# A preparing pass over the context, dissolved into two cross attentions of a four-layer kernel

## The reference, cut to what matters

```
L0 cross attention: 16 heads of 64, keys and values projected from ctx
L1 cross attention:  8 heads of 64, keys and values projected from layernorm(ctx) * g + b
L2 cross attention, linear: k = ctx @ wk, v = ctx @ wv                   (256 x 256 each)
    k' = (relu(layernorm(k) * g + b) + 1e-6) * mask
    v' = (layernorm(v) * g + b) * mask
    kv = k'^T v' over all 12544 rows, and the sum of k' over the rows; both small
```

## Time and profile before

| What | Value |
|---|---|
| median of 3 executions | 3282.53 us (3282.21 to 3284.53) |
| profiled execution, its own time | 3287.21 us |
| its span, first to last instruction | 3285.6 us |
| busy PE, DVE, ACT, POOL | 2809.3, 1830.1, 1530.2, 475.2 us |
| mean granted TensorE clock | 0.927 |
| preparing stage | about 3.5 to 347.4 us |
| first cross attention | about 348 to 1533 us |
| second cross attention | about 1737 to 2365 us |
| HBM read, written | 201.27 MB, 38.80 MB |

### The profile page before, as it was taken

The page is one execution under the profiler, slowest core; times in us unless marked ns, Lnnn a source line. Parts: engine busy times, 40 slices in busy tenths (PEclk is TensorE's granted clock), DMA queues, the critical chain, the costliest instruction groups (busy, mean ns, idle before and its releaser), DMA issues. The chain is left out here.

```text
span 3285.6 us, 72653 instructions
## 1 busy us (share of the span) xinstructions
PE 2809.3 (86%) x26026; PEld 2244.3 (68%) x26026; DVE 1830.1 (56%) x5010; ACT 1530.2 (47%) x3126; POOL 475.2 (14%) x915
## 2 busy tenths in 40 slices
PE   6788699999999999995666999999767559999973
PEld 5666588888888888884345888888546446777752
DVE  7999455555555555554574555555453347565625
ACT  5777455555555555552443555555300002444441
POOL 3333111111111111100012222222000011000000
PEclk9999899999999999997787999999869687999985
DMA  3334311111111111001442111110124264334210
GB/s 112 119 119 118 114 57 42 39 36 35 35 35 35 35 35 35 29 2 36 163 156 86 35 35 35 35 35 22 55 110 166 107 248 128 123 114 125 75 35 18
DMA packets 128243, 244.15 MB, mean 74 GB/s; under 512 B 16448, under 2 KB 89168, under 8 KB 122576
## 3 DMA queue, kind: packets, MB, share of 16 engines
q1 hardware_dynamic: 95696, 208.26, 18.9%
q10 hardware_dynamic: 28672, 19.27, 1.9%
q0 software_dynamic: 3584, 12.58, 1.2%
HBM read 201.27 MB, written 38.80 MB: 73 GB/s over the span
## 5 line engine op out<-in xcount | busy, mean ns | idle before, releaser
L340 PE MATMUL l0x_psum<-l0x_fast 128*128 128x448 f32 x1344 | 331.6, 383 | 20.3 <-DVE l0x_fast L545 12.8
L470 ACT ACTIVATE l0x_sbuf<-l0x_sbuf 128x896 f32<-128x896 f32 x224 | 233.2, 1041 | 231.2 <-DVE l0x_sbuf L565 231.2
L1447 DVE CUSTOM_DVE_ANT_0 l3x_sbuf<-l3x_psum,l3x_fast,l3x_sbuf 128x896 f32<-128x896 f32 x224 | 253.4, 1150 | 140.0 <-PE l3x_psum L1294 135.6
L1378 ACT ACTIVATE l3x_sbuf<-l3x_psum 128x512 f32<-128x512 f32 x392 | 213.7, 596 | 220.7 <-PE l3x_psum L1313 220.2
L355 PE MATMUL l0x_psum<-l0x_fast 128*128 128x512 f32 x1176 | 310.5, 401 | 0.9 <-POOL l0x_fast L625 0.9
L551 DVE TENSOR_TENSOR l0x_fast<-l0x_psum,l0x_fast 128x448 fp32r<-128x448 f32 x224 | 140.0, 625 | 298.3 <-ACT l0x_fast L450 298.3
L340 PEld LDWEIGHTS l0x_psum<-l0x_fast 128*128 128x128 f32 x1344 | 237.2, 190 | 41.8 <-issue 12.9
L565 DVE CUSTOM_DVE_ANT_0 l0x_sbuf<-l0x_psum,l0x_sbuf 128x896 f32<-128x896 f32 x224 | 248.9, 1149 | 25.6 <-PE l0x_psum L369 25.6
L186 PE MATMUL prep_psum<-prep_sbuf 128*128 128x256 f32 x784 | 196.8, 395 | 70.0 <-DMA prep_sbuf<-in_ctxT 63.8
L576 DVE COPY l0x_sbuf<-l0x_psum 128x384 f32<-128x384 f32 x224 | 124.8, 557 | 236.3 <-PE l0x_psum L386 236.3
L355 PEld LDWEIGHTS l0x_psum<-l0x_fast 128*128 128x128 f32 x1176 | 213.5, 188 | 57.3 <-issue 16.7
(11 more groups left out here) (700 smaller groups left out, 5625.7 us busy)
## 6 DMA issues: line engine op xcount, KB each, us to landing
l3x_fast<-ctx_high SPq DMA_DIRECT2D x112, 224.0 KB, 3.7
l1f_sbuf<-in_L_ffn_W SPq DMA_DIRECT2D x16, 1024.0 KB, 6.8
l2f_sbuf<-in_L_ffn_W SPq DMA_DIRECT2D x16, 1024.0 KB, 6.9
prep_sbuf<-in_ctx_rows SPq DMA_DIRECT2D x98, 128.0 KB, 2.1
prep_sbuf<-in_ctxT SPq DMA_DIRECT2D x98, 128.0 KB, 2.5
xnT<-prep_sbuf ACTq DMA_DIRECT2D x98, 128.0 KB, 2.3
l0x_sbuf<-in_ctxT SPq DMA_DIRECT2D x14, 896.0 KB, 6.2
ctx_high<-l0x_fast SPq DMA_DIRECT2D x14, 896.0 KB, 7.8
```

The lines of the kernel that those rows point to most:

```text
L340: mm = pe.matmul(ps[:, 0:width], self.wk[w][:, c, pr * T:(pr + 1) * T], x[:, c, lo:lo + width], start=(j == 0), stop=(j == len(products) - 1))
L470: act.activation(self.p[:, (2 * m + a) % 4, 0:width], self.sm[:, a, 0:width], ACT.Exp, scale=-1.0, bias=self.negm[:, n % 2, 2 * pr + a:2 * ...
L1378: act.activation(p[:, u % 4, :, :, :].rearrange("p h a t -> p (h a t)"), ps_t[slot["tiles", u]][:, :], ACT.Exp).then_inc(s.sem("p"), 1)
L1447: dve.tensor_tensor_reduce(junk[:, a, :].rearrange("p (i c) -> p i c", i=2), ps_s[a][:, :, 0:HALF], bias[:, n * CH:(n + 1) * CH].bitcast(F ...
```

## The change

The preparing stage is gone from `STAGES`. Its work moves:

- **Into the first cross attention**, in a new class `ContextSide`. Per tile one column group of 512 columns in f32r, key and value weights of the linear attention side by side (three products of two halves, as for the values), one in each of the steps pr 0 to 6. ACT empties it. DVE takes three `bn_stats` at the end of that step. Twice a chunk (tiles 0 to 3 and 4 to 6) DVE aggregates, forms the inverse roots by a shift, a constant and three Newton steps (`dve_scales`, ends of pr 4 and pr 7), and normalises keys and values (`dve_normal`, ends of pr 5 and of pr 0 of the next chunk). POOL applies gain, shift and relu to the keys of the batch (ends of pr 5 and pr 0). PE forms the sums of a batch at the end of pr 7 and of pr 3 of the next chunk, in one of the two shared banks, and DVE adds that bank to a running total one step later, behind its first L551.
- The output weights `wo` get the place of the side's keys and values, so they are loaded when the last sums are done. Raw weights lie in other buffers, and `v` is kept for four pairs of heads at a time instead of eight.
- **Into the second cross attention**: it reads `ctxT` and the means and inverse spreads of the rows, which the first one writes to HBM (49 KB each). Per chunk SP loads them to all partitions (448 KB each), and POOL does three operations on each of the two halves of 896 columns (`norm_part`), at pr 1 for the chunk after the next. At the start POOL does one half of chunk 0 and DVE the other, and POOL all of chunk 1 before its first `diff`.
- In both attentions the groups of chunk 0 are no longer ahead of step 0, but in the steps 0 and 1 (and for the first attention's second half of the heads in 2 to 5).

```diff
+        for u in range(self.M // 4):
+            n, e = divmod(u, P // 4)
+            steps = range(4 * u - 2, 4 * u + 2) if u else range(2)
+            mine = [(n, t, e) for t in range(self.tiles(n))]
             for i, m in enumerate(steps):
                 lo, hi = i * len(mine) // len(steps), (i + 1) * len(mine) // len(steps)
-                self.plan[m] = [len(self.groups) + k for k in range(lo, hi)]
+                self.plan.setdefault(m, []).extend(("v", len(self.groups) + k, 0) for k in range(lo, hi))
             self.groups += mine
-        uses = [("k", 0, i) for i in range(len(self.halves(0)))] + [("v", g, 0) for g in self.plan[-1]]
+            self.ready.append(len(self.groups))
+        if side is not None:
+            for n in range(NCH):
+                for t in range(CT):
+                    self.plan.setdefault(P * n + t, []).append(("side", n * CT + t, 0))
+        uses = [("k", 0, i) for i in range(len(self.halves(0)))]
         for m in range(self.M + 2):
             keys = [("k", m + 1, i) for i in range(self.parts_of(m + 1))]
-            groups = [("v", g, 0) for g in self.plan.get(m, [])]
+            groups = self.plan.get(m, [])
             turns = [("turn", m - 2, 0)] if m >= 2 else []
-            uses += keys[:1] + groups[:1] + keys[1:] + groups[1:] + turns
+            sums = [("sum", b, 0) for b in side.sums_at(m)] if side is not None else []
+            uses += keys[:1] + groups[:1] + keys[1:] + groups[1:] + turns + sums
         self.slot = {use: i % 2 for i, use in enumerate(uses)}
         self.before = {use: uses[i - 2] for i, use in enumerate(uses) if i >= 2}
 
...
-        for g in self.plan[-1]:
-            self.pe_group(pe, g)
...
+            if self.side is not None:
+                for b in self.side.sums_at(m):
+                    self.side.pe_sum(pe, b, self.pe_slot(pe, "sum", b, 0))
...
-        act.wait_ge(s.sem("raw_in"), (n + 1) * 16)
+        if self.norm_dram is None:
+            act.wait_ge(s.sem("raw_in"), (n + 1) * 16)
+        else:
+            act.wait_ge(s.sem("normed"), 2 * n + 2)
...
             if m + 1 < self.M:
                 self.dve_keys(dve, m + 1, 0)
+            if self.side is not None:
+                for b in self.side.sums_at(m - 1):
+                    self.side.dve_summed(dve, b, self.ps_kv[self.slot["sum", b, 0]])
...
                 self.dve_turned(dve, m - 1, 1)
             if m >= 2:
                 self.dve_acc(dve, m - 2)
+            if self.side is not None:
+                self.side.dve_step(dve, m)
...
+    def norm_part(self, eng, n, c):
+        s = self.s
+        eng.wait_ge(s.sem("raw_in"), (n + 1) * 16)
+        eng.wait_ge(s.sem("mean_in"), (n + 1) * 16)
+        eng.wait_ge(s.sem("rstd_in"), (n + 1) * 16)
+        eng.wait_ge(s.sem("gain_in"), 32)
+        part = self.raw[:, c, :]
+        eng.tensor_tensor(part, part, self.mean[:, :], ALU.subtract).then_inc(s.sem(f"centered{c}"), 1)
+        eng.wait_ge(s.sem(f"centered{c}"), n + 1)
+        eng.tensor_tensor(part, part, self.rstd[:, :], ALU.mult).then_inc(s.sem(f"scaled{c}"), 1)
+        eng.wait_ge(s.sem(f"scaled{c}"), n + 1)
+        eng.tensor_scalar(part, part, self.gain[:, 0, c:c + 1], self.gain[:, 1, c:c + 1], ALU.mult, ALU.add).then_inc(s.sem("normed"), 1)
+
+    def pool_norm(self, pool, n):
+        for c in range(DC):
+            self.norm_part(pool, n, c)
...
+            if pr == 1 and self.norm_dram is not None and n + 2 < NCH:
+                self.pool_norm(pool, n + 2)
+            if self.side is not None:
+                self.side.pool_step(pool, m)
+        if self.side is not None:
+            self.side.pool_step(pool, self.M)
...
+    def sums_at(m):
+        n, pr = divmod(m, 8)
+        if pr == 7 and 0 <= n < NCH:
+            return [2 * n]
+        if (pr == 3 and 0 < n < NCH) or (pr == 1 and n == NCH):
+            return [2 * n - 1]
+        return []
+
+    @staticmethod
+    def tiles(b):
+        return range(4) if b % 2 == 0 else range(4, CT)
...
+    def act_in(self, act, i, ps):
+        s = self.s
+        n, t = divmod(i, CT)
+        act.wait_ge(s.sem("side_ps"), i + 1)
+        self.wait(act, "sum_ps", 2 * n - (1 if t < 4 else 0))
+        act.activation(self.kv[:, t, :].rearrange("p (b e) -> p b e", b=2)[:, :, 0:D],
...
+    def dve_step(self, dve, m):
+        n, pr = divmod(m, 8)
+        if n < NCH and pr < CT:
+            self.dve_moments(dve, n, pr)
+        if n < NCH and pr == 4:
+            self.dve_scales(dve, 2 * n)
+        if n < NCH and pr == 5:
+            self.dve_normal(dve, 2 * n)
+        if n < NCH and pr == 7:
+            self.dve_scales(dve, 2 * n + 1)
+        if n > 0 and pr == 0:
+            self.dve_normal(dve, 2 * n - 1)
+
+    def dve_moments(self, dve, n, t):
+        s = self.s
+        dve.wait_ge(s.sem("side"), n * CT + t + 1)
+        dve.wait_ge(s.sem("rows_in"), (n + 1) * 16)
+        self.wait(dve, "side_mv", n * 3 * CT - (9 if t < 4 else 0))
+        dve.bn_stats(self.st[:, t, 0, :], self.k(t)).then_inc(s.sem("side_st"), 1)
+        dve.bn_stats(self.st[:, t, 1, :], self.v(t)).then_inc(s.sem("side_st"), 1)
+        dve.bn_stats(self.st[:, t, 2, :], self.rows[:, t, :]).then_inc(s.sem("side_seen"), 1)
+    def dve_scales(self, dve, b):
+        s = self.s
+        mine, n = slice(self.tiles(b)[0], self.tiles(b)[-1] + 1), b // 2
+        dve.wait_ge(s.sem("side_st"), 2 * self.seen(b))
+        dve.wait_ge(s.sem("side_seen"), self.seen(b))
+        self.wait(dve, "side_v", b - 1)
+        for t in self.tiles(b):
+            for i in range(3):
+                dve.bn_aggr(self.mv[:, t, i, :], self.st[:, t, i, :]).then_inc(s.sem("side_mv"), 1)
+        dve.wait_ge(s.sem("side_mv"), 3 * self.seen(b))
+        dve.wait_ge(s.sem("side_ready"), 3)
+        link = linker(dve, s.sem("side_steps"), 12 * b)
+        var, half, r = self.var[:, mine, :], self.half[:, mine, :], self.r[:, mine, :]
+        link(dve.tensor_tensor(var, self.mv[:, mine, :, 1], self.eps[:, mine, :], ALU.add))
+        link(dve.tensor_scalar(half.bitcast(I32), var.bitcast(I32), 1, None, ALU.logical_shift_right))
+        link(dve.tensor_scalar(r.bitcast(I32), half.bitcast(I32), -1.0, 1597463007.0, ALU.mult, ALU.add))
+        for _ in range(3):
+            link(dve.scalar_tensor_tensor(out=half, in0=r, scalar=-0.5, in1=r, op0=ALU.mult, op1=ALU.mult))
+            link(dve.tensor_tensor(half, half, var, ALU.mult))
+            link(dve.scalar_tensor_tensor(out=r, in0=half, scalar=1.5, in1=r, op0=ALU.add, op1=ALU.mult))
+        at = slice(n * CT + mine.start, n * CT + mine.stop)
+        if b == 0:
+            dve.wait_ge(s.sem("side_squares"), 1)
+        dve.tensor_tensor(self.scale[:, mine], self.r[:, mine, 1], self.masks[:, at, 1], ALU.mult).then_inc(s.sem("side_scale"), 1)
+        dve.tensor_copy(self.stats[:, 0, at], self.mv[:, mine, 2, 0]).then_inc(s.sem("side_stats"), 1)
+        dve.tensor_copy(self.stats[:, 1, at], self.r[:, mine, 2]).then_inc(s.sem("side_stats"), 1)
+
+    def dve_normal(self, dve, b):
+        s = self.s
+        dve.wait_ge(s.sem("side_scale"), b + 1)
+        for t in self.tiles(b):
+            ins = dve.tensor_scalar(self.k(t), self.k(t), self.mv[:, t, 0, 0:1], self.r[:, t, 0:1], ALU.subtract, ALU.mult)
+        ins.then_inc(s.sem("side_z"), 1)
+        for t in self.tiles(b):
+            ins = dve.tensor_scalar(self.v(t), self.v(t), self.mv[:, t, 1, 0:1], self.scale[:, t:t + 1], ALU.subtract, ALU.mult)
+        ins.then_inc(s.sem("side_v"), 1)
+
+    def dve_summed(self, dve, b, ps):
+        s = self.s
+        dve.wait_ge(s.sem("sum_ps"), b + 1)
+        dve.wait_ge(s.sem("side_ready"), 3)
+        self.wait(dve, "summed", b)
+        dve.tensor_tensor(self.total[:, :, :], self.total[:, :, :], ps[:, 0:260].rearrange("p (c e) -> p c e", c=2),
+                          ALU.add).then_inc(s.sem("summed"), 1)
...
+    def pool_step(self, pool, m):
+        s = self.s
+        n, pr = divmod(m, 8)
+        if pr == 4:
+            self.wait(pool, "sum_ps", 2 * n)
+            for at in (D, self.W + D):
+                pool.tensor_copy(self.kv[:, :, at:at + 2], self.masks[:, n * CT:(n + 1) * CT, :]).then_inc(s.sem("side_masks"), 1)
+        b = 2 * n if pr == 5 else 2 * n - 1
+        if pr == 5 or (pr == 0 and n > 0):
+            k = self.kv[:, self.tiles(b)[0]:self.tiles(b)[-1] + 1, 0:D]
+            gain, shift = (v[:, :].unsqueeze(1).to_broadcast([128, len(self.tiles(b)), D]) for v in (self.g, self.b))
+            pool.wait_ge(s.sem("side_z"), b + 1)
+            pool.tensor_tensor(k, k, gain, ALU.mult).then_inc(s.sem("side_gained"), 1)
+            pool.wait_ge(s.sem("side_gained"), b + 1)
+            pool.tensor_tensor(k, k, shift, ALU.add).then_inc(s.sem("side_shifted"), 1)
+            pool.wait_ge(s.sem("side_shifted"), b + 1)
+            pool.tensor_scalar(k, k, 0.0, 1e-6, ALU.max, ALU.add).then_inc(s.sem("side_k"), 1)
+
+    def pe_sum(self, pe, b, ps):
```

(27 more changed lines are left out.)

408 lines of the change are left out of this document (160 added, 248 removed).

## The result

The changed kernel takes 3545.5 us (median of 4 runs, 3539.9 to 3554.8), the kernel before 3283.5 (4 runs, 3282.2 to 3288.1): a ratio of 1.080, 95% interval 1.077 to 1.082. It is slower by 262 us. The forecast was 3317, with a range of 3230 to 3390: the sign was right, the size was not.

The account below looks back on a forecast made before the run. DVE bounds the preparing stage, PE both cross attentions. Stage removed -343.9, first attention +329, second attention's POOL work +44, its start +6: +35 us, 3322, or 3317 against the median; range 3230 to 3390.

Parts of the forecast that it names:

- the forecast's 13.2 us of products: First attention, PE: 98 side groups at 1.36 us, 133 us, and 392 sum products, 52 us; together +185.
- forecast (10.2, and the 0.9 of before): First attention's seams: DVE work and bank order make PE wait 10.2 us a chunk, 141 us in all.
- 3.7 us of DVE work at pr 5 and 3.0 at pr 0: First attention's seams: moments and normalising on DVE, making PE wait 2.0 us at pr 5 and 0.6 at pr 0.
- POOL's batches: First attention: three operations of 1024 or 768 elements, some 7 us in a step of 11 or more, costing nothing.
- costs of nothing: First attention: ACT's 98 copies, POOL's side operations and SP's row loads were all claimed to add no time.
- my bounds for that term: First attention's seam waits: lower 7 us a chunk (98 in all), upper 13 (181), by how far DVE operations overlap.
- a forecast of 3.7: Second attention: POOL's 10.5 us of normalising delays `diff` and `alpha`; PE waits 3.7 us a chunk, 44 in 12 chunks.
- The waits at pr 4, pr 7 and pr 3: First attention's seams: PE waits 3.2 us for DVE's scales chain, 2.4 and 2.0 for the sum's bank.
- the seam's room of 1.7 us: Between two steps of the first attention, DVE has 1.7 us free; work beyond it delays PE one for one.
- the bank's order: First attention, pr 3: PE waits 2.0 us for the sum's bank, freed only behind L551, though DVE is idle enough.
- rival 1: First attention's seams: DVE overlaps its short operations, waits 98 us instead of 141, kernel 3274; chance 0.32.
- Rival 2: Second attention: POOL's batch is the dear one, at L634's price, +54 us, kernel 3371; chance 0.15.

Follow-up runs that it names:

- experiment 5: Changed kernel with DVE's side work moved from the step's end into its 3.0 us idle place in mid-step, moments one step later: 3321.6 us, ratio 1.012.
- experiment 6: Changed kernel with 20 extra PE products, results overwritten, at each of the two long waits (behind pr 5 and pr 0): 3508.7 us, ratio 1.069.
- Experiment 2: Changed kernel with POOL's key batch (gain, shift, max) left out but for a max on two columns: 3408.4 us, ratio 1.038.
- Experiment 1: Changed kernel with POOL's key batch also waiting for the value normalising of the same batch: 3415.7 us, ratio 1.040.
- experiment 3: Changed kernel with POOL's key batch behind the value normalising and the odd batch's normalising moved from pr 0 to pr 1: 3372.4 us, ratio 1.027.
- experiment 4: Changed kernel with the sums' products ahead of the turn and DVE's total ahead of the accumulators: 3509.6 us, ratio 1.069.
- experiment 8: Changed kernel with key batch behind values, sums ahead of the turn, side work in mid-step and second attention's POOL batch halved: 3203.6 us, ratio 0.975.

## Why the prediction was wrong

**The bookkeeping of a chunk.** Before, a chunk of the first attention took 80.9 us with 0.9 of waits. To the remaining 80.0 I add the forecast's 13.2 us of products (7 groups at 1.36, 28 sum products at 0.133) and the waits of PE for other engines that the rows show, those from 0.3 us up, as a mean of six chunks:

| kernel | period | waits | rest |
|---|---|---|---|
| forecast (10.2, and the 0.9 of before) | 104.3 | 11.1 | 0 |
| changed kernel | 119.5 | 19.7 | 6.5 |
| sums first (4) | 116.1 | 17.5 | 5.4 |
| key batch behind the values (1) | 109.2 | 13.3 | 2.7 |
| odd batch at pr 1 too (3) | 105.9 | 11.1 | 1.6 |
| side work in mid-step (5) | 102.4 | 9.4 | -0.2 |
| all (8) | 99.1 | 6.1 | -0.2 |

The rest closes to nothing in the kernels whose waits stay about 2 us, so the products' term was right, to about a microsecond. It may still be some tenths too high: in experiment 5 the six loads at 645.28 take 2.21, and the window from 645 to 650 has a clock of 0.66. The rest grows with the long waits, and experiment 6 shows what most of it is: with a period of 115.5, waits of 10.9 and the fillers' own 8.8 us taken off, the rest there is 2.6 in place of 6.5. That is the clock, which PE gets back late.

**The term that failed** is the one of 3.7 us of DVE work at pr 5 and 3.0 at pr 0, together with "POOL's batches" under the costs of nothing. I took 0.33 us for a normalising operation, from rows in which POOL did nothing beside it, and I looked at POOL's batch only for its length and for whom it delays in its own queue. Experiment 2 shows that this half was right: its length costs about 7 us in all. The other half, what it does to an operation on DVE that starts a tenth of a microsecond later, I didn't ask. Measured, the waits are 6.70 and 5.71 where the forecast had 2.0 and 1.5 (its 0.6 and the 0.9 that stood there before): 8.9 us a chunk, 125 in 14. Experiment 1, which takes away the overlap with POOL's key batch and nothing else, gives 130 us back with the clock behind those waits; experiment 3, which takes away the one with L705 and shifts the odd batch by a step, another 43. Without the overlap the two waits are 1.8 (forecast 2.0) and, at the odd batch's two seams together, 2.0 (forecast 1.5).

I had even cited the two-port mode of `tensor_scalar` for a price, to reject it. The price was rightly rejected (for the 0.33 that I took, experiment 3 has an operation every 0.31 to 0.33), but what POOL does to such an operation was the question that mattered, and my bounds for that term (7 to 13 us a chunk in all) had no POOL in them. The nearest rows before the change, and the earlier trace rows, don't show it, since none of those normalising operations started beside an operation of POOL on SBUF. But the trace before had the effect on another line of the preparing stage, and I didn't look for it there (DVE, then POOL):

```profile
201.01 0.41 DVE L971 BATCH_NORM_STATS2 prep_sbuf<-prep_sbuf 128x6 f32<-128x256 f32 x1
201.35 0.46 DVE L974 TENSOR_TENSOR prep_sbuf<-prep_sbuf 128x3 f32<-128x3 f32 x1
```

```profile
201.15 0.64 POOL L1030 TENSOR_TENSOR prep_sbuf<-prep_sbuf 128x256 f32<-128x256 f32 x1
```

L974 has three elements and two inputs in SBUF. It ends at 201.81, L1030 at 201.79. Of the 98 L974, 74 started while POOL was working: they took 0.30 to 0.46 us and ended 0.015 to 0.022 us behind POOL's instruction. The other 24 took 0.14 to 0.16. L971, with one input, keeps 0.41 to 0.43 in both cases. So the trace that the forecast was read from already showed that an operation on DVE can stand until POOL's instruction ends, and that not every form does. It is not the normalising form, so the size of the term could still not be read from it.

**The second term that failed** is one that was not there: the clock. Every wait was charged its own length. It is 6.5 us a chunk, 91 in 14, in the first attention, of which experiment 6 gave 3.9 a chunk back; for the remainder only the slow loads behind the waits of 2.85 and 2.48 speak, no run. With the 125 that is 216, and since the periods of the first chunks are shorter than the settled one (109.7 and 116.4 of 119.5), it fits the 197 missed there. It is also more than half of what was missed in the second, where a chunk became 6.4 us longer with a forecast of 3.7 and PE's wait was 4.7; the products right behind that wait take 1.7 us more than a step earlier (the keys 2.59 for 1.48, the transposes 0.87 and 0.85 for 0.60 and 0.49).

**What held.** The waits at pr 4, pr 7 and pr 3 (2.8, 2.5, 2.0 for 3.2, 2.4, 2.0), and with them the seam's room of 1.7 us and the bank's order, which experiment 4 showed as a cost of its own; the products; that POOL's batch stalls ACT's `alpha` in the second attention, by its 10.9 us; that ACT's copies and SP's loads are hidden in the first attention, where the waits shown above name DVE alone. Without the overlap the forecast's chunk came out (105.9 for 105; its own terms add up to 104.3, and the table has 1.6 of clock that it didn't have, so the last part of the agreement is luck). Of the rivals, rival 1 (faster) failed on its own condition, waits under 7.3 a chunk: experiment 8 has 6.1 and the changed kernel 19.7, both with the 0.9 of before. Rival 2 asked whether the (mult, add) operation on POOL goes at L634's price: it doesn't, but the (max, add) of the key batch does, 3.6 us for 1024 elements, where it cost nothing.
